# Routing by sorted chunks in the second layer's experts, and block-wise attention with early lengths in the last FFN

## The reference

```python
        scores = jax.nn.softmax(logits, axis=-1).T
        topk_weight, topk_idx = jax.lax.top_k(scores, C)
        xg = flat_x[topk_idx]
...
        flat_out = jnp.zeros_like(flat_x).at[topk_idx.reshape(-1)].add(eo.reshape(-1, d))
```

```python
            q = l2norm(q) * qs
            k = l2norm(k) * ksc
            q, k = rotary_xpos(q, k)
            o = local_attention(q, k, v)
```

## Time and profile before

| | before |
|---|---|
| median of 3 runs | 1983.05 us (1978.85 to 1985.16) |
| profiled execution | 1986.88 us, of which the span is 1985.0 us |
| busy: TensorE, weight load, VectorE, ScalarE, GpSimd | 71%, 53%, 61%, 35%, 22% of the span |
| routing of the layer 1 experts | 992.8 to 1050.4, 57.6 us |
| projection, first and second block of the last FFN | 24.0 and 24.5 us |
| rotation with lengths | 1605.5 to 1661.1 and 1803.3 to 1858.9, 55.6 us each |
| attention | 1661.1 to 1725.0 and 1858.9 to 1922.8, 63.9 us each |

### The profile page before, as it was taken

The page is one execution under the profiler, slowest core; times in us unless marked ns, Lnnn a source line. Parts: engine busy times, 40 slices in busy tenths (PEclk is TensorE's granted clock), DMA queues, the critical chain, the costliest instruction groups (busy, mean ns, idle before and its releaser), DMA issues. The chain is left out here.

```text
span 1985.0 us, 23801 instructions
## 1 busy us (share of the span) xinstructions
PE 1402.2 (71%) x8374; PEld 1058.3 (53%) x8374; DVE 1202.4 (61%) x2327; ACT 695.9 (35%) x1421; POOL 439.8 (22%) x451
## 2 busy tenths in 40 slices
PE   2688888888775995854727938677259747964795
PEld 2466666666644663732617926556237625832573
DVE  4599999999455675135686465343467367436744
ACT  1366566656222562321311220032024233423341
POOL 0366665655112001021002210000010041004000
PEclk8699999998877897876968959589679876977697
DMA  5101111010010101600004400000200000000000
GB/s 179 49 27 38 39 34 38 27 39 15 1 55 0 33 1 32 195 15 0 1 12 147 133 0 1 1 0 1 85 0 1 1 0 1 1 0 0 0 1 11
DMA packets 31413, 60.36 MB, mean 30 GB/s; under 512 B 6720, under 2 KB 17984, under 8 KB 31040
## 3 DMA queue, kind: packets, MB, share of 16 engines
q1 hardware_dynamic: 30272, 56.62, 8.9%
q0 software_dynamic: 1024, 2.23, 0.5%
HBM read 54.65 MB, written 4.18 MB: 30 GB/s over the span
## 5 line engine op out<-in xcount | busy, mean ns | idle before, releaser
L187 POOL TENSOR_TENSOR rstd<-spread,minus_half 128x4 f32<-128x4 f32 x36 | 36.8, 1024 | 961.6 <-DVE spread L169 961.6
L911 PE MATMUL l0h_scores<-l0h_k_rot,l0h_q_slots 128*128 128x128 f32 (+1 forms) x1024 | 205.8, 348 | 0.0
L911 PEld LDWEIGHTS l0h_scores<-l0h_k_rot,l0h_q_slots 128*128 128x128 f32 x1024 | 168.7, 206 | 13.1
L1115 POOL TENSOR_TENSOR l0h_k_part<-large_weights,l0h_sines 128x512 f32<-128x512 f32 x64 | 83.1, 1298 | 219.5 <-PE l0h_scores L911 126.3
L991 ACT ACTIVATE l0h_scores<-l0h_scores,l0h_top 128x128 f32<-128x128 f32 (+1 forms) x256 | 100.6, 393 | 27.8 <-DVE l0h_top L1068 27.6
L887 PE MATMUL l0h_projected<-XT,l0h_wq 128*128 128x256 f32 x256 | 71.0, 401 | 18.3 <-DVE l0h_q_rot L1055 9.2
L1062 DVE TENSOR_TENSOR l0h_q_slots<-l0h_q_rot,l0h_chosen 128x1024 f32<-128x1024 f32 x64 | 78.4, 1225 | 7.0 <-DVE l0h_q_rot L1059 0.5
L1116 POOL TENSOR_TENSOR l0h_k_rot<-large_weights,l0h_cosines 128x512 f32<-128x512 f32 x64 | 81.9, 1280 | 0.0
L901 PE MATMUL l0h_scores<-l0h_key_masks,l0h_query_picks 4*128 4x128 bf16 (+1 forms) x256 | 44.6, 255 | 50.6 <-DVE l0h_probs L1085 50.5
L1068 DVE TENSOR_REDUCE l0h_top<-l0h_scores 128x2 f32<-128x256 f32 (+1 forms) x128 | 65.0, 546 | 6.5 <-PE l0h_scores L911 6.5
L1422 ACT ACTIVATE l0n_probs<-l0n_scores,l0n_top 128x256 f32<-128x256 f32 x128 | 53.9, 483 | 38.9 <-DVE l0n_top L1453 38.8
(11 more groups left out here) (708 smaller groups left out, 3674.6 us busy)
## 6 DMA issues: line engine op xcount, KB each, us to landing
l1e_experts<-in_l_experts SPq DMA_DIRECT2D x16, 768.0 KB, 4.4
l0e_experts<-in_l_experts SPq DMA_DIRECT2D x15, 578.0 KB
l0h_chosen<-l0h_chosen_dram SPq DMA_DIRECT2D x64, 128.0 KB, 2.9
l0h_pos<-l0h_pos_dram SPq DMA_DIRECT2D x64, 64.0 KB, 2.0
small_weights<-in_w_l_ffn SPq DMA_DIRECT2D x1, 4016.0 KB, 12.0
large_weights<-in_w_l_xattn SPq DMA_DIRECT2D x1, 2632.0 KB, 9.1
l0h_wq<-in_l_wq SPq DMA_DIRECT2D x16, 128.0 KB, 2.9
large_weights<-in_w_l_attn SPq DMA_DIRECT2D x2, 512.0 KB, 5.5
```

Of the source, the lines that this page charges most:

```text
L911: mm = nc.tensor.matmul(at[:, slot], q_slots[:, s % 2, slot, part, i * P:(i + 1) * P], k_rot[:, s % 2, part, 0:KEYS[i][1]], start=False, s ...
L1115: nc.gpsimd.tensor_tensor(k_part[:], source, at_batch(sines, s), ALU.mult)
```

## The change

In `l1_ffn_route` the probabilities are turned once, as they lie, to 128 rows of 128: row (t, e) holds the values of expert e in token tile t. Half of the rows are negated, and 16 rounds of `max` and `match_replace` sort every row completely. Eight DMAs bring the eight lists of each expert onto 16 partitions. Half-cleaner steps merge them: one pair of instructions leaves four lists, seven pairs sort these, one pair leaves two, seven pairs sort these, and one instruction leaves the 128 largest, whose least is the threshold. It is turned to all partitions, every value is compared with it, and nine bf16 products count the ranks of values above and equal, from which five instructions make `slot`.

In the last FFN a new block `l3_ffn_project` squares q and k out of PSUM beside the copies, sums the squares per head on VectorE, which also copies the values, and ends with a power of -0.5 on GpSimd over 2 x 8 x 8 = 128 numbers per partition. `l3_ffn_rotate` has no lengths; only k is multiplied with its inverse length, q's goes as a scale into the exponents. In the same block two DMAs copy the values, shifted by 64 tokens, to a second tile `late`. A new block `l3_ffn_attend` replaces `attention`: in each of 16 units every window of 64 queries is scored against its own 128 keys only, so that a unit always has 512 columns; the exponents are four instructions of 128 columns that read PSUM; the weights of the last product are 64 columns wide, for two windows in turn. The masks `far_own` and `far_before` give way to `far` and `far_first`, built by three memsets and four selects in a chain.

```diff
@@ l1_ffn_route
 sync:
+                sp.wait_ge(sorted_ready.sem, sorted_ready.base + 1)
+                for t in range(T):
+                    sp.dma_start(lists[:, t, :], in_order[t * E1:(t + 1) * E1, :]).then_inc(listed, 16)
 tensor:
-                for t in range(T):
-                    mm = nc.tensor.transpose(by_expert_ps[:, t * P:(t + 1) * P], exps[:, t, :], k.ident[:])
+                nc.tensor.transpose(chunks_ps[:], exps[:].rearrange("p t e -> p (t e)"), k.ident[:])\
+                    .then_inc(turned_ready.sem, 1)
...
-                for t in range(T):
-                    mm = nc.tensor.transpose(slot_ps[:, t, :], place[:, t * P:(t + 1) * P], k.ident[0:E1, 0:E1])
+                nc.tensor.transpose(least_ps[:], best[:], k.ident[0:E1, 0:E1]).then_inc(least_turned, 1)
+                pe.wait_ge(marked_ready, 1)
+                nc.tensor.matmul(ranks_ps[:, 0:T, :], k.above[:], marked[:], start=True, stop=False,
+                                 skip_group_check=True)
                 for t in range(T):
+                    mm = nc.tensor.matmul(ranks_ps[:, t + 1:, :], k.ones16[:],
+                                          bc(marked[:, t, :].unsqueeze(1), [P, T - t, 2 * E1]), start=False,
+                                          stop=(t == T - 1), skip_group_check=True)
 vector:
-                link(v, nc.vector.tensor_copy(left[:], by_expert_ps[:]))
-                for _ in range(CAP // 8):
-                    link(v, nc.vector.max(best[:], left[:]))
-                    link(v, nc.vector.match_replace(left[:], best[:], left[:], -1.0))
-                link(v, nc.vector.tensor_scalar(chosen[:], left[:], 0.0, None, ALU.is_lt))
-                link(v, nc.vector.tensor_tensor_scan(place[:], chosen[:], chosen[:], 0.0, ALU.add, ALU.max))
-                link(v, nc.vector.tensor_tensor(place[:], place[:], chosen[:], ALU.mult))
-                nc.vector.tensor_scalar(place[:], place[:], 1.0, None, ALU.subtract).then_inc(places_ready, 1)
+                link(v, nc.vector.tensor_scalar(left[:], chunks_ps[:], sign[:], None, ALU.mult))
+                for r in range(P // 8):
+                    best8 = in_order[:, 8 * r:8 * r + 8]
+                    last = nc.vector.max(best8, left[:])
+                    if 8 * r + 8 < P:
+                        link(v, last)
+                        link(v, nc.vector.match_replace(left[:], best8, left[:], -2.0))
+                last.then_inc(sorted_ready.sem, 1)
...
+                def sort(lists_of, at):
+                    step = P // 2
+                    while step:
+                        of, to = (x.rearrange("e l (g o s) -> e l g o s", o=2, s=step)
+                                  for x in (merged[:, at, 0:lists_of], merged[:, 1 - at, 0:lists_of]))
+                        nc.vector.tensor_tensor(to[:, :, :, 0], of[:, :, :, 0], of[:, :, :, 1], ALU.max)
+                        link(v, nc.vector.tensor_tensor(to[:, :, :, 1], of[:, :, :, 0], of[:, :, :, 1], ALU.min))
+                        at, step = 1 - at, step // 2
+                    return at
...
+                v.wait_ge(listed, 16 * T)
+                merge(merged[:, 0], lists[:, 0:4], lists[:, 4:8], 2)
+                at = sort(4, 0)
+                merge(merged[:, 1 - at], merged[:, at, 0:2], merged[:, at, 2:4], 1)
+                at = sort(2, 1 - at)
+                link(v, nc.vector.scalar_tensor_tensor(best[:], merged[:, at, 1, :], -1.0, merged[:, at, 0, :], ALU.mult,
+                                                       ALU.max))
+                link(v, nc.vector.tensor_reduce(least[:], best[:], AX.X, ALU.min))
...
-            attention(k, tag + "_att", [unit(t, g) for t in range(T) for g in range(2)], 8.0)
+                l3_ffn_project(k, tag, W, table, shifted, rows, tables, flat, values, late, q_t, k_padded, inverse)
+                l3_ffn_rotate(k, tag, tables, rows, {"q": q_t[:], "k": k_t}, flat, late, inverse, heads_out)
+            l3_ffn_attend(k, tag, q_t, k_padded, flat, late, inverse, far, far_first, heads_out)
@@ l3_ffn_project (new), scalar, vector, gpsimd
+                    nc.scalar.activation(squares[:, part, c % 2].rearrange("p a d -> p (a d)"), areas[:, n % 4, :],
+                                         ACT.Square).then_inc(squared.sem, 1)
+                    nc.scalar.copy(rows["qk"[part]][:, 2 * c:2 * c + 2], both(areas[:, n % 4, :]))\
+                        .then_inc(by_scalar.sem, 1)
...
+                for c in range(T // 2):
+                    for part in range(2):
+                        v.wait_ge(squared.sem, squared.base + 2 * c + part + 1)
+                        last = nc.vector.tensor_reduce(sums[:, part, 2 * c:2 * c + 2].rearrange("p t h -> p (t h)"),
+                                                       squares[:, part, c % 2], AX.X, ALU.add)
+                    v.wait_ge(projected.sem, projected.base + 3 * c + 3)
+                    nc.vector.tensor_copy(values[:, 2 * c:2 * c + 2, :, 0:DL].rearrange("p t h d -> p (t h) d"),
...
+                nc.vector.tensor_scalar(sums[:, 0], sums[:, 0], QK_SCALE ** -2, (1e-12 / QK_SCALE) ** 2, ALU.mult, ALU.max)
+                nc.vector.tensor_scalar(sums[:, 1], sums[:, 1], 1e-24, None, ALU.max).then_inc(clipped.sem, 1)
...
+                g.wait_ge(clipped.sem, clipped.base + 1)
+                nc.gpsimd.tensor_tensor(inverse[:], sums[:], half[:], ALU.pow)
@@ l3_ffn_rotate
+            @block.sync
+            def _(sp):
+                full, one = T * HL * (DL + 1), HL * (DL + 1)
+                sp.dma_start(late[WINDOW:P, 0:full], flat[0:WINDOW, 0:full]).then_inc(late_ready.sem, 16)
+                sp.dma_start(late[0:WINDOW, one:full], flat[WINDOW:P, 0:full - one]).then_inc(late_ready.sem, 16)
+                sp.wait_ge(late_ready.sem, late_ready.base + 32)
...
-                for x in "qk":
-                    nc.scalar.activation(squares[x], heads[x], ACT.Square).then_inc(squared.sem, 1)
-                act.wait_ge(summed.sem, summed.base + 1)
-                nc.scalar.activation(length[:], length[:], ACT.Sqrt).then_inc(rooted.sem, 1)
...
-                for n, x in enumerate("qk"):
-                    v.wait_ge(squared.sem, squared.base + n + 1)
-                    last = nc.vector.tensor_reduce(length[:, n, :], squares[x], AX.X, ALU.add)
-                last.then_inc(summed.sem, 1)
-                v.wait_ge(rooted.sem, rooted.base + 1)
-                link(v, nc.vector.tensor_scalar(length[:], length[:], 1e-12, None, ALU.max))
-                link(v, nc.vector.reciprocal(length[:], length[:]))
...
-                    link(v, nc.vector.tensor_tensor(one, one, part_of(t), ALU.add))
-                    lengths = length[:, "qk".index(x), t * HL:(t + 1) * HL].unsqueeze(2)
-                    nc.vector.tensor_tensor(one, one, bc(lengths, [P, HL, DL]), ALU.mult).then_inc(tile_ready.sem, 1)
+                    last = nc.vector.tensor_tensor(one, one, part_of(t), ALU.add)
+                    if x == "k":
+                        link(v, last)
+                        last = nc.vector.tensor_tensor(one, one, bc(inverse[:, 1, t].unsqueeze(2), [P, HL, DL]), ALU.mult)
+                    last.then_inc(tile_ready.sem, 1)
@@ l3_ffn_attend (new)
+                    for o in range(2):
+                        nc.tensor.matmul(out[:, o, 0:2 * P].rearrange("p (y w) -> p y w", y=2),
+                                         not_seen[:].rearrange("p c w -> p (c w)"), masks, start=True, stop=False,
+                                         skip_group_check=True)
+                    for y in range(2):
+                        for c in range(2):
+                            at = t * P + c * WINDOW
+                            for o in range(2):
+                                part = slice(o * DL, (o + 1) * DL)
+                                mm = nc.tensor.matmul(out[c * WINDOW:(c + 1) * WINDOW, o, y * P:(y + 1) * P],
+                                                      q_t[part, 2 * g + y, at:at + WINDOW],
+                                                      k_padded[part, 2 * g + y, at:at + P], start=False, stop=True,
+                                                      skip_group_check=True)
...
+                    for x in range(4):
+                        mm = nc.tensor.transpose(turned[:, u % 2, x * P:(x + 1) * P], probs[:, u % 2, x], k.ident[:])
...
+                            for c, rows_of in enumerate((late, flat)):
+                                mm = nc.tensor.matmul(outs[c * WINDOW:(c + 1) * WINDOW, u % 2, first:first + P],
+                                                      probs_t[:, u % 2, x * P + c * WINDOW:x * P + (c + 1) * WINDOW],
+                                                      rows_of[:, (t * HL + 4 * g + 2 * y + o) * (DL + 1):][:, 0:P],
+                                                      start=True, stop=True, skip_group_check=True)
...
```

(13 more changed lines are left out.)

308 lines of the change are left out of this document (207 added, 101 removed).

## The result

| | before | after |
|---|---|---|
| median of 4 runs each, side by side | 1982.97 us (1978.85 to 1985.16) | 1957.12 us (1954.58 to 1962.47) |
| profiled execution | 1986.9 us | 1955.0 us, span 1952.9 |
| routing, subtraction to last `slot` | 53.2 us | 35.7 us |
| projection from its first product, first and second block | 24.0, 24.1 us | 47.2, 45.6 us |
| rotation | 55.6, 55.6 us | 44.4, 44.4 us |

The ratio is 0.9876, with a 95% interval of 0.9847 to 0.9904: 25.9 us faster, where 16.5 were forecast. (Each stage runs to the first instruction of the next one, so the change of block is in it. By that measure the second projection of before is 24.1 us, from 1779.24 to 1803.31, and not 24.5.)

A forecast was written before the change was run, and what follows sets the result against it. No single engine bounds it: VectorE routing, VectorE with GpSimd rotation, TensorE projection and attention. -18.3 + 0.4 + 2 x (21.6 - 11.0 - 9.9) = -16.5 us, a median of 1966.5; own range 1950 to 1986, 8 in 10 1930 to 1986.

The forecast's parts named there:

- Routing: Expert routing, bound by VectorE's sorting: 128-column rounds, list transfers, merging and tail end at 1031.7 against 1049.96, -18.3 us.
- the issue of the lists: Routing: eight DMAs at 0.43 us an issue, the last landing 2.1 us after its issue, 5.1 us on the path.
- The tail: End of the routing: transpose and copy, marks, nine bf16 products and five operations, 5.2 us.
- The masks: Mask building: seven chained instructions in place of five partly free ones, +0.4 us, once.
- lists late: Rival in the routing: lists land after 12 us in place of 2.1, giving 1976.5 us; chance 0.10.
- Projection: Last FFN's projection: TensorE stays the bound, then GpSimd's power of 20.3 us stands uncovered; +21.6 us per block.
- the rival of the cheap power: End of projection: power on 128 columns costs near that on 12, each block 18.0 us shorter, 1930.5; chance 0.15.
- Rotation: Last FFN's rotation: lengths go, GpSimd's parts of q come into the open; 44.6 against 55.6 us, -11.0 per block.
- Attention: Last FFN's attention, bound by TensorE: units of 2.8 us, total 53.9 against 63.8 us, -9.9 per block.
- small tiles don't overlap: Rival in the attention: tiles of one PSUM bank wait for each other, 4.7 us a unit, 2023 us; chance 0.12.
- The sum of 2.5: Attention: TensorE's work per unit if scores overlap four at a time (0.5 us); ScalarE's loop would set 2.6.
- 9.9 + 1.2: Attention's start at low clock: 9.9 us as before plus 1.2 for twice the score instructions.

The follow-up runs named there:

- e1: The kernel before with only the new routing (`l1_ffn_route`) of the changed kernel; 1966.6 us, ratio 0.9917 to the kernel before.
- e10: Changed kernel with four of the eight list transfers issued from ScalarE's queue; one execution: first merge 4.1 us after the last `max` in place of 6.3.
- e3: Changed kernel with a root on ScalarE and a reciprocal on VectorE in place of GpSimd's power; 1921.1 us, ratio 0.9699 to the kernel before.
- e4: Changed kernel with the power in four pieces of 32 columns under the projection, each once its sums are clipped; 1929.65 us, ratio 0.9733.
- e7: Changed kernel with q's tiles multiplied by lengths again in the rotation (k's factors); 1970.66 us, ratio 0.9932 to the kernel before.
- e8: e3 with GpSimd making q's sine parts during the projection, leaving k's in the rotation; 1905.85 us, ratio 0.9616 to the kernel before.
- e9: e8 with the attention's copy of the turned probabilities moved from ScalarE to VectorE; 1899.07 us, ratio 0.9573 to the kernel before.
- e5: Changed kernel with one exponential of 512 columns a unit in place of four, constant scale, no shift; 1947.3 us, ratio 0.9823 to the kernel before.
- e6: Changed kernel with the attention's score loop over the two halves of the rows moved from innermost to outermost; 1960.44 us, ratio 0.9893.

## Why the prediction was right, point by point

**Routing** (-18.3 forecast; -17.4 in the trace, -16.8 by e1). A round took 0.715 us where 0.69 was worked out from the line through the earlier trace rows, and the merging 11.2 where 11.6. The mis-sized term was the issue of the lists. I took 0.43 us each from three large transfers; these small ones take 0.64 each, so 6.3 us lie between the last `max` and the merge, not 5.1. The tail gave 0.6 back (4.6, not 5.2). The masks cost 0.7 us where 0.4 was added. e10 shows that this is issue and not landing. The rival "lists late", with its 12 us of landing, is ruled out: they landed in 1.8.

**Projection** (+21.6 a block, where the terms themselves add to 21.5; +23.2 and +21.5). The power is 20.78 us, where 20.3 was drawn through 4 and 12 columns. e3 and e4 show that nothing covered it and that its price goes by columns. This kills the rival of the cheap power. The Trainium skill's 2.6 cycles an element (GPSIMD Engine Reference, section 3.1), measured on an add, would by the estimate have made it 0.3 us; the power took seventy times that, so an add's price does not carry over to it, and the measurement decides. The first block's 1.7 us more go with TensorE's clock, which was granted in full later (0.50 over its first 4 us and 0.73 over the next, where before had 0.60 and 1.00 in the same places). The change alone doesn't decide that: e4, e7, e8 and e9 have its projection too, and there the same stretches show 0.64 or 0.65, and 1.00.

**Rotation** (44.6 us forecast, 44.4 measured in both blocks). The sum held, the late transfers were hidden, and the pairs went at 1.14 us as the two engines took turns. One sentence beside it was wrong: "So eight multiplications less on VectorE bring nothing by themselves". The sum itself counted VectorE's 40 instructions, all of them in a row; eight more are 5.6 us at its 0.70 and 9.1 at its 1.14. e7 measured 5.5 a block in the rotation and 6.8 in the whole. VectorE is busy for 40.06 of the 44.44 us, which fits that each of its instructions is on the path.

**Attention** (-9.9 a block; -15.1 and -13.6). This is where the forecast was off: by 8.9 us in the two blocks, which is more than the 8.2 between the forecast for the last FFN without its masks (+1.4) and its trace (-6.8). Three things stand in it.
- The unit was right: 2.74 us against 2.8. But the reason was half right. I had placed the value between the loops of TensorE (2.5 to 3.0) and ScalarE (2.6). TensorE's own is 2.43 (e5) and ScalarE's sets it (e5 and e9), since the four exponentials take 1.51 us (they start 0.345 apart, and the last one's own time is 0.465), not the 4 x 0.336 = 1.34 of the earlier trace rows.
- The scores overlap four at a time: 16 instructions in 0.67 us, where eight of the two-way form took 0.71. The rival "small tiles don't overlap" is ruled out. The Trainium skill's four independent tiles of 64x64 (TensorEngine Tiling (Array Packing), Tiling Modes) is what the trace shows. The drain at a change of mode that this section states fits the 0.21 and 0.17 us of idle where the form of the loads changes (e5). The sum of 2.5 that the prediction gave for this case is near TensorE's 2.43; its unit of 2.6, set by ScalarE, came out at 2.74.
- The start was mis-sized: 11.1 us at low clock, worked out as "9.9 + 1.2". Taking 15 x 2.74 and 0.8 for the end from the stage leaves 6.9 us in the first block and 8.5 in the second. Against 11.1 that is 3.4 a block of the 4.5 that were missing, and the unit's 0.06 x 15 is 0.9 more. The second turns show the same directly. They begin 6.9 and 8.6 us after the stage does (at 1647.87 and 1840.60), where before it was 9.3 (1661.13 to 1670.47):

```profile
1654.81 0.66 PE L3257 MATMUL l3f0a_turned<-ident,l3f0a_probs 128*128 128x128 f32 x4 [0.24 <-ACT l3f0a_probs L3294]
...
1849.23 0.66 PE L3257 MATMUL l3f1a_turned<-ident,l3f1a_probs 128*128 128x128 f32 x4
```

  Three things went into that. The 1.2 us added for twice the score instructions never came: at the clock of 0.50 sixteen of them take 1.13 us, and the eight of before took 1.23. The 9.9 of before was no fixed price of a start either, since it held the scores of a unit with 256 keys. These are the scores of the third unit, before and in the changed kernel, both at 0.50:

```profile
1666.95 2.08 PE L3022 MATMUL l3f_att_scores<-l3f_k_t,l3f_q_t 64*128 64x256 f32 x8
...
1846.29 1.13 PE L3246 MATMUL l3f1a_scores<-l3f_k_t,l3f_q_t 64*64 64x128 f32 x16
```

  And in the first block the full clock came after 3.3 us and not after 8.6, which is the 1.7 us between the two blocks. Nothing in my sum stood for that; it is luck of the profiled execution. In the ten attentions of the changed kernel, e3, e6, e7 and e8, whose units are alike, the second turn comes after 8.6 us in seven, after 8.2 in one and after 6.9 or 7.0 in two.

**The sum.** The forecast was 9.4 us too high, within its own range; the start of the attention is 7 of them in these traces, and 5 where both blocks have the 8.6 us of most runs. By the traces the stages that were changed gain 23.5 us (17.4 + 6.8 - 0.7) against the 16.5 of the sum. The other 2.4 of the 25.9 are in no changed stage, and less than the interval of the ratio leaves open. Its main statement, that in the last FFN the power eats the gain, held: without it (e3) the last FFN gains 44 us, not 8.

## What to carry to other kernels

Price an instruction by its operation and its shape from rows, and if only small shapes are there, draw the line through two of them; before a costly one is put where nothing else runs, ask which idle engine has it in two cheap ones. When a tile loop has several engines in a ring, take the unit with each engine's work taken away in turn: the difference is what moving a copy to another engine can bring, no more. And work that leaves the path of one stage (the parts under the projection) also stops slowing its neighbour there.

## What the runs showed of the hardware

- GpSimd's power on two f32 tiles of 128 partitions: 0.40 us and 0.159 a column, from 4 to 128 columns. A multiplication of 256 columns on the same engine takes 0.73 (e8).
- Instructions on 64*64 tiles start 0.027 us apart (16 in 0.67 us, of which the last one's own are 0.27), in both orders of the four tiles that were tried. The two-way form's were 0.063 apart by the same working.
- TensorE's granted clock goes from 1.2 to 2.4 GHz at different points of the same code. The stretches of the changed kernel's two attentions, from 1647.87 and from 1840.60, show it (two of the first, the last of the second):

```profile
1650.00:1651.00 1.00, 1.00 (x17) 0.72 (x16) 0.44 (x2) 0.49 (x2) 0.00 (x0) 0.50 0.00 0
1651.00:1652.00 1.00, 0.12 (x4) 0.00 (x0) 0.78 (x2) 1.00 (x3) 0.00 (x0) 0.91 0.00 0
...
1846.60:1848.60 2.00, 2.00 (x28) 1.67 (x22) 0.85 (x2) 1.36 (x4) 0.00 (x0) 0.50 0.00 0
```

  The first has the full clock 3.3 us after its start, the second 8.6 us after, with the same rotation behind it and TensorE busy for all but a few hundredths of the first 3 us in both. The first stage is 1.7 us shorter. What decides between the two I did not find.
- Eight transfers of 8 KB from SBUF to SBUF take 0.64 us each to issue on SyncE's queue, three loads of the experts' weights 0.43 each. What makes the difference no run shows.
- VectorE and GpSimd at work on SBUF tiles side by side take 1.09 to 1.21 and 1.09 us where they take 0.69 and 0.73 apart (rotation, e8).
